# Query product from the transposed raw input and scaled afterwards, with the fourth layernorm's sums on ScalarE

## The reference, cut to what matters

```python
x = x + xattn(layernorm(x), ctx, ctx)      # q, k, v: relu(a @ W + b); relu(q k^T) / sqrt(512) + mask; relu(. @ v)
x = x + ffn(layernorm(x))                  # rows and weight quantised in blocks of 32 to a 6-bit float grid
x = x + mix(layernorm(x), ctx)             # x @ W1^T + mean part + b
x = x + experts(layernorm(x))              # 16 experts, each on the 128 tokens that its gate likes best
```

## Time and profile before

| | us |
|---|---|
| three runs | 745.37, 745.30, 744.03; median 745.3 |
| span of the profiled execution | 743.2 |
| PE busy | 716.2 (96%) |
| PEld busy | 624.9 (84%) |
| DVE busy | 521.6 (70%) |
| POOL busy | 420.4 (57%) |
| ACT busy | 401.9 (54%) |

### The profile page before, as it was taken

The page is one execution under the profiler, slowest core; times in us unless marked ns, Lnnn a source line. Parts: engine busy times, 40 slices in busy tenths (PEclk is TensorE's granted clock), DMA queues, the critical chain, the costliest instruction groups (busy, mean ns, idle before and its releaser), DMA issues.

```text
span 743.2 us, 12766 instructions
## 1 busy us (share of the span) xinstructions
PE 716.2 (96%) x4513; PEld 624.9 (84%) x4513; DVE 521.6 (70%) x978; ACT 401.9 (54%) x680; POOL 420.4 (57%) x621
## 2 busy tenths in 40 slices
...
GB/s 317 256 30 15 43 86 62 88 86 58 88 79 82 71 58 108 52 60 44 49 45 264 322 396 279 149 391 186 222 370 185 185 330 293 289 266 167 142 86 58
DMA packets 61671, 118.04 MB, mean 159 GB/s; under 512 B 6056, under 2 KB 7464, under 8 KB 61608
## 3 DMA queue, kind: packets, MB, share of 16 engines
...
...
## 4 chain that ended last, share of the span: by engine, by line
PE 84%; issue 6%; DMA 4%; DVE 3%; ACT 2%; POOL 1%; POOLq 0%; SPq 0%; DVEq 0%; ACTq 0%
PE bank L354 39%; PE banks L354 9%; PE bank L361 6%; PE bank L994 6%; PE banks L861 4%; PE banks L867 4%; DMA out<-y,ids 3%; PE banks L871 2%; PE banks L994 2%; PE banks L872 2%; PE banks L1423 1%; PE banks L1028 1%; PE bank L1318 1%; PE bank L1041 1%; DMA out<-x 1%
## 5 line engine op out<-in xcount | busy, mean ns | idle before, releaser
L2844 POOL DMA_INDIRECT out<-y,ids x24 | 46.1, 1922 | 157.4 <-DVE y L2555 155.5
L1973 DVE TENSOR_TENSOR w_l<-w_raw,w_h 128x2048 fp32r<-128x2048 f32 x35 | 80.1, 2291 | 63.2 <-ACT w_h L1496 49.4
L1961 DVE BATCH_NORM_STATS2 bn<-x 128x6 f32<-128x512 f32 x113 | 77.7, 688 | 8.2 <-DMA x<-x 5.4
L1496 ACT ACTIVATE w_h<-w_raw 128x2048 fp32r<-128x2048 f32 x36 | 68.5, 1918 | 7.2 <-DMA w_raw<-w 7.2
L1892 ACT ACTIVATE h<-bank,b 128x512 f32<-128x512 f32 x48 | 33.0, 688 | 62.5 <-PE bank L354 57.8
L1973 DVE TENSOR_TENSOR hT_l<-h,hT_h 128x512 fp32r<-128x512 f32 x48 | 33.0, 689 | 39.8 <-ACT hT_h L1898 37.7
L354 PE MATMUL bank<-tokT_h,w_h 128*128 128x256 f32 x188 | 55.1, 293 | 0.0
L2607 POOL TENSOR_SCALAR rstd<-mean_var 128x1 f32<-128x1 f32 x108 | 25.7, 238 | 50.9 <-DVE mean_var L1966 42.6
L354 PE MATMUL bank<-tokT_h,w_l 128*128 128x256 f32 x188 | 53.2, 283 | 0.0
L354 PE MATMUL bank<-tokT_l,w_h 128*128 128x256 f32 x188 | 53.2, 283 | 0.0
L354 PE MATMUL bank<-wf_h,xdT_h 128*128 128x512 f32 x128 | 52.6, 411 | 0.0
...
## 6 DMA issues: line engine op xcount, KB each, us to landing
...
x<-x SPq DMA_DIRECT2D x32, 256.0 KB, 2.7
out<-x SPq DMA_DIRECT2D x32, 256.0 KB, 2.0
xn<-xn SPq DMA_DIRECT2D x32, 256.0 KB
mask<-mask_t SPq DMA_DIRECT2D x8, 256.0 KB, 3.4
...
```

What stands on the lines that cost most here:

```text
L1496: act.activation(dst, src, ACT.Copy).then_inc(sem, 1)
L1961: dve.bn_stats(bn6[which][:, j % 2, :], src[:, :]).then_inc(sem_bn[which], 1)
L1973: dve.tensor_tensor(dst, src, hi_part, ALU.subtract).then_inc(sem, 1)
L2844: pool.indirect_dma_start(out=out_rows, out_offset=bass.IndirectOffsetOnAxis(ap=ids[:, r:r + 1], axis=0), in_=y[e % 2][b][:, :], in_offset ...
```

## The change

It uses that layernorm is a shift and a scale of each token. If the mean over its input features is taken out of each column of the query weight, the product of the raw `x` with it is the product of `x - mean` with the weight, and each token's 1/sqrt(var + eps) can be multiplied in afterwards.

- The host hands in `x` also transposed (`x_t`). SP loads it by groups (1 MB, 8 times) into the bytes of the low half of `xT1`. `xt_hi` (ACT, two instructions of 128x1024 per group, turns k % 4 = 0 and 1) makes the high part. The low part is made of three pieces of 128x512 on POOL (turns k % 4 = 0, 1, 2, behind `q_lo`) and one on DVE (k % 4 = 2); for groups 0 and 1 it is one instruction of 128x2048 on DVE. `t1`, `norm1`, `hi1`, `lo1` and six warm-up matmuls are gone.
- Four fp32 matmuls at the start give the weight's means, two DVE instructions subtract them.
- `rstd1` is made for four tiles at once (POOL, turns k % 4 = 1), written to DRAM and loaded back as a row on all partitions (`rb`). For group 0 this goes through PE and ACT.
- `scaled` (DVE, new, one per chunk) multiplies the product's bank by `rb` into `q32`; `q_relu` then works on `q32` in SBUF, high part first, then `q32` in place.
- `SUMMED` covers tiles 0 to 29: 22 tiles' sums move from DVE to ACT.
- In the loop, ACT's `hi2(k)` now stands ahead of `q_relu`, and POOL's `rstd4(k - 3)` behind `xd(k)` and `x1b(k)`, no longer ahead of them.
- At the start the DMAs, and the lists of steps on ACT, DVE and POOL, have another order (`wsum` is now ahead of the fourth `q_relu`).

The diff, cut to its core (from top to bottom: rules for all engines, SP, PE, ACT, DVE, POOL):

```diff
-    SUMMED = range(N - 10, N - 2)
+    SUMMED = range(0, N - 2)
...
+    def halves_of_group(k):
+        g, half = (k + 8) // GRP, k % GRP
+        return (g, half) if 2 <= g < G and half < 2 else None
+    def pool_piece(k):
+        g, c = (k + 8) // GRP, k % GRP
+        return (g, c) if 2 <= g < G and c < 3 else None
...
+        def load_xt(g):
+            if g >= 2:
+                sp.wait_ge(sm.p_q, GRP * (g - 1))
+            sp.dma_start(xt_raw[g % 2][:, :, :], chunked(io.x_t)[:, :, g * GT:(g + 1) * GT])\
+                .then_inc(sem_xt[g % 2], 16)
+        def store_r1(g):
+            sp.wait_ge(sm.g_r1, g + 1)
+            sp.dma_start(io.r1[g * GT:(g + 1) * GT].rearrange("(t p) -> p t", p=P), r1[:, g % 3, :],
+                         allow_slow_non_contiguous=True).then_inc(sm.r1_out, 16)
+        def load_rb(g):
+            sp.wait_ge(sm.r1_out, 16 * g)
+            sp.wait_ge(sm.d_z, GRP * g)
+            sp.dma_start(rb[:, :], rows_on_all(io.r1[g * GT:(g + 1) * GT], GT)).then_inc(sm.rb_in, 16)
...
-        def t1(j):
-            pe.wait_ge(sm.a_xn1, j + 1)
...
-            four_transposes(pe, bank1(j), xn1).then_inc(sm.p_t1, 1)
...
             if n == 0:
                 pe.wait_ge(sm.a_set, A["wq1"])
                 pe.wait_ge(sm.d_set, V["wq1"])
-            pe.wait_ge(sm.d_lo1, GRP * (g + 1))
+            pe.wait_ge(sm.d_xtl, g + 1)
+            if g >= 2:
+                pe.wait_ge(sm.g_xtl, 3 * (g - 1))
             if n >= 2:
-                pe.wait_ge(sm.a_q, n - 1)
+                pe.wait_ge(sm.d_z, n - 1)
             if n == 5:
...
+        def query_weight_means():
+            for d in range(C):
+                if d % 2 == 0:
+                    pe.wait_ge(sm.c_wq0 if d == 0 else sm.c_wq1, 16)
+                if d == 0:
+                    pe.wait_ge(sm.g_set, GS["mean"])
+                last = pe.matmul(ps_tb[:, :], mean_w[:, :], stage[0][:, d, :], start=(d == 0), stop=(d == C - 1))
+            last.then_inc(sm.p_set, 1)
+        def first_rows():
+            pe.wait_ge(sm.c_ident, 16)
+            pe.wait_ge(sm.g_r1, 1)
+            for t in range(GRP):
+                last = pe.transpose(ps_ta[:, t * P:(t + 1) * P], r1[:, 0, t:t + 1].to_broadcast([P, P]), ident[:, :])
+            last.then_inc(sm.p_set, 1)
...
-        t1(0)
-        warm_up(3)
...
+        query_weight_means()
...
+        first_rows()
...
-            if valid(k + 9):
-                t1(k + 9)
...
-        def norm1(j):
-            act.wait_ge(sm.p_t1, j)
-            norm(0, j, x_in[j % XR], xn1, sm.a_xn1, sm.g_r1)
...
-        def hi1(j):
...
-            hi(sm.a_hi1, xT1[j // GRP % 2][0][:, :, cols(j)], in4(bank1(j)))
+        def xt_hi(g, half):
+            act.wait_ge(sem_xt[g % 2], 16 * (g // 2 + 1))
+            part = slice(2 * half, 2 * half + 2)
+            hi(sm.a_xth, xT1[g % 2][0][:, part, :], xt_raw[g % 2][:, part, :])
...
         def q_relu(g, c, n):
...
-            act.wait_ge(sm.p_q, n + 1)
-            if n >= 2:
-                act.wait_ge(sm.g_qlo, n - 1)
-            act.activation(q32[n % 2][:, :], ps_q[n % 2][:, :], ACT.Relu, bias=bq[:, c:c + 1])
+            act.wait_ge(sm.d_z, n + 1)
             act.wait_ge(sm.p_s, g)
-            act.activation(q_h[:, c, :], ps_q[n % 2][:, :], ACT.Relu, bias=bq[:, c:c + 1]).then_inc(sm.a_q, 1)
+            act.activation(q_h[:, c, :], q32[n % 2][:, :], ACT.Relu, bias=bq[:, c:c + 1])
+            act.activation(q32[n % 2][:, :], q32[n % 2][:, :], ACT.Relu, bias=bq[:, c:c + 1]).then_inc(sm.a_q, 1)
...
         setup("k2")
         setup("k3")
+        setup("rb0")
         q_relu(*q_of(0))
-        hi1(4)
-        norm1(5)
+        xt_hi(1, 0)
         q_relu(*q_of(1))
-        hi1(5)
-        norm1(6)
+        xt_hi(1, 1)
         q_relu(*q_of(2))
-        hi1(6)
-        norm1(7)
+        setup("wsum")
         q_relu(*q_of(3))
-        hi1(7)
-        setup("wsum")
...
-            j = k + 9
-            if valid(j) and k >= 1:
-                hi1(j)
+            if halves_of_group(k) is not None:
+                xt_hi(*halves_of_group(k))
             if valid(k - 3) and not drain(k):
                 norm4(k - 3)
             g = scores_of(k)
             if g is not None and not scores_first(k):
                 s_relu(g)
-            if q_units(k):
-                q_relu(*q_units(k)[0])
             j = k
             if valid(j):
                 act.wait_ge(sm.p_t2, j + 1)
                 act.wait_ge(sm.p_f, j)
                 hi(sm.a_hi2, xd_h[:, :, :], in4(ps_tb))
+            if q_units(k):
+                q_relu(*q_units(k)[0])
             if fourth_later(k - 4):
...
-        def lo1(j):
-            i = j // GRP % 2
-            dve.wait_ge(sm.a_hi1, j + 1)
-            lo(sm.d_lo1, xT1[i][1][:, :, cols(j)], in4(bank1(j)), xT1[i][0][:, :, cols(j)])
+        def xt_lo(g):
+            dve.wait_ge(sm.a_xth, 2 * g + 2)
+            part = slice(0, C) if g < 2 else slice(C - 1, C)
+            lo(sm.d_xtl, xT1[g % 2][1][:, part, :], xt_raw[g % 2][:, part, :], xT1[g % 2][0][:, part, :])
+        def scaled(g, c, n):
+            dve.wait_ge(sm.p_q, n + 1)
+            if g == 0:
+                dve.wait_ge(sm.a_set, A["rb0"])
+            else:
+                dve.wait_ge(sm.rb_in, 16 * g)
+            if n >= 2:
+                dve.wait_ge(sm.g_qlo, n - 1)
+            dve.tensor_tensor(q32[n % 2][:, :], ps_q[n % 2][:, :], rb[:, :], ALU.mult).then_inc(sm.d_z, 1)
         def s_mask(g):
...
+        setup("wq0")
+        setup("wq1")
+        xt_lo(0)
         stats1(0)
         stats1(1)
         stats1(2)
         stats1(3)
-        lo1(0)
-        lo1(1)
-        lo1(2)
-        lo1(3)
         setup("wgc")
-        setup("wq0")
-        setup("wq1")
         stats1(4)
+        scaled(*q_of(0))
         stats1(5)
         setup("wf scales")
+        scaled(*q_of(1))
         stats1(6)
         stats1(7)
-        lo1(4)
         setup("wf8_0")
+        scaled(*q_of(2))
         setup("wf8_1")
-        lo1(5)
+        setup("wf8_2")
+        scaled(*q_of(3))
+        setup("wf8_3")
+        xt_lo(1)
         stats1(8)
         stats1(9)
-        lo1(6)
-        setup("wf8_2")
-        setup("wf8_3")
-        lo1(7)
         setup("va0")
         setup("v0")
         s_mask(0)
...
-            j = k + 9
-            if valid(j) and k >= 3:
-                lo1(j)
...
                 stats1(j)
+            if q_units(k):
+                scaled(*q_units(k)[0])
+            if k % GRP == 2 and 2 <= (k + 6) // GRP < G:
+                xt_lo((k + 6) // GRP)
...
+        def rstd1(g):
+            r, m = r1[:, g % 3, :], mv[0][:, GRP * g % 12:GRP * g % 12 + GRP, 1]
+            pool.wait_ge(sm.d_st1, GRP * (g + 1))
+            if g >= 4:
+                pool.wait_ge(sm.r1_out, 16 * (g - 3))
+            then(pool.tensor_scalar(r, m, LN_EPS, None, ALU.add))
+            pool.tensor_tensor(r, r, eps_exp[:, :].to_broadcast([P, GRP]), ALU.pow).then_inc(sm.g_r1, 1)
+        def xt_lo(g, c):
+            pool.wait_ge(sm.a_xth, 2 * g + 1 + c // 2)
+            lo(sm.g_xtl, xT1[g % 2][1][:, c, :], xt_raw[g % 2][:, c, :], xT1[g % 2][0][:, c, :])
...
-            if valid(k - 3) and not drain(k):
-                rstd_of(3, k - 3, sm.d_st4, sm.g_r4)
...
+            if valid(k - 3) and not drain(k):
+                rstd_of(3, k - 3, sm.d_st4, sm.g_r4)
...
                 s_lo(g)
-            if valid(k + 10):
-                rstd1(k + 10)
             if k == 1:
                 q_lo(*q_of(4))
             if not drain(k):
                 for unit in q_units(k):
                     q_lo(*unit)
+            if valid(k + 10) and (k + 11) % GRP == 0:
+                rstd1((k + 10) // GRP)
+            if pool_piece(k) is not None:
+                xt_lo(*pool_piece(k))
```

154 lines of the change are left out of this document (64 added, 90 removed).

## The result

The changed kernel takes 814.63 us (median of 4 runs, 810.57 to 816.94), the kernel before 745.04 in the same sessions: a ratio of 1.093, 95% interval [1.0896, 1.0958]. It is slower, as forecast, but by 69.6 us instead of 29, outside the range of 754 to 791.

The account below looks back on a forecast made before the run. PE bound the kernel before; a closed POOL-ACT-POOL chain would bind the changed loop. Span 743.2 + 2.8 (start) + 27.25 (five groups) - 1.5 (end) = 771.8, with 2.1 to the median 774 us; range 754 to 791.

Parts of the forecast that it names:

- the three waits named: Loop, turns 4 to 24: PE waits for POOL's xd, POOL for ACT's q_relu before q_lo, ACT for POOL's rstd4 before norm4.
- A: Rival for the loop: the chain has slack and PE remains the bound; 737.5 us, or 739.6 as a median; chance 0.10.
- B: Rival for the loop: the chain holds only in part, a group takes 45.3 to 47, time 747 to 755 us; chance 0.08.
- The chain of a plain turn: Loop, xd to next xd through POOL, ACT, POOL: 3.72 + 2.67 + 5.55 = 11.95 us, where PE needs 10.1.
- `xs64` 168.62 to 168.99 = 0.37: POOL, last step of the plain turn's chain: xs64 counts 0.37 us up to the next xd.
- the power on 128x4: POOL's rstd1 in turns k % 4 = 1: power taken as 1.1 us, with 0.4 for the addition, turn 13.45.
- The score turn: Turn k % 4 = 3: s_relu, mask, high part, sums and scaled stand ahead of q_relu; 13.4 us in all.
- 50.75: Group of four turns, 2 x 11.95 + 13.45 + 13.4 us instead of 45.30: 5.45 more, five times.
- The start: Before turn 4: first scores 4.2 us later, turns 1 to 3 give back 1.4; +2.8 at turn 4, bounds 0 and 7.
- I take half, 1.1: Start, DVE: second chunk's scaled behind the ffn weight's reductions, 2.25 us each, costs nothing or one; half taken.
- The end: From turn 24: the orders change, the chain ends, and t2(24) comes sooner after xd(24); -1.5 us.
- C: Rival: row rb, through DRAM, arrives 3 us late for a group's first chunk in five groups; 789 us; chance 0.07.

Follow-up runs that it names:

- e2_rstd4_ahead: Changed kernel, but on POOL rstd4(k-3) stands ahead of xs64 and xd again, ACT's order left as changed: 775.62 us, ratio 1.042.
- e8_mix_first: Changed kernel, but on POOL mix_bias stands ahead of rstd2, so it does not run beside DVE's scale: 832.07 us, one run.
- e4_start: Changed kernel, start reordered: second group's xt_hi and wsum behind q_relu, second scaled ahead of weight reductions, later q_lo ahead of dequantisation: 811.61 us, 1.091.
- e9_srelu_first: Changed kernel, but in score turns ACT does s_relu ahead of norm4 and not behind it: 805.67 us, ratio 1.082.
- e12_settled: Changed kernel with rstd4 and s_relu earlier, low-part pieces on DVE, start reordered, xt_hi at turn's end, sums of tiles 17 to 21 on DVE: 765.82 us, 1.029.

## Why the prediction was right or wrong

- **The bound and the side: right.** PE is no longer full, each of the three waits named stands where it was put, and cutting the chain at either end gives back 33 to 39 us. A (PE stays the bound) falls with these two runs, B (the chain holds only in part) with the group of 55.9. By size the span came out 40.4 us longer than the 771.8 of the sum: 24.5 of it lie in turns 4 to 23 (+51.7, past the upper bound of +38.5), 10.2 before them and 5.9 in turns 24 to 26.
- **The chain of a plain turn: right up to `xs64`, then mis-sized.** In turn 10 it is 6.79 to `q_lo` against 6.39, and 5.10 from there to `xs64` against 5.18; the power on 128x4 takes 1.04 to 1.05 (1.1 taken). The step that failed is "`xs64` 168.62 to 168.99 = 0.37": in each of the twenty turns `xd` comes 1.33 to 1.34 behind `xs64`, because it waits for DVE. That is 0.96 a turn and 19 us in all, the largest part of the miss. Before, the three instructions of `rstd4` stood between `mix_bias` and `xs64` and covered DVE's steps; the forecast took `xd` to depend on POOL alone there. With `rstd4` back in its place (e2_rstd4_ahead) most of these waits are gone. In the three turns without scores DVE is late since its scale takes 1.16 to 1.21 beside `mix_bias`; e8_mix_first shows that it is this neighbour.
- **The score turn: mis-sized by 1.0 to 3.3.** Up to `q_lo` turn 11 takes 9.04, as the sum had it (its terms add up to 9.2, not to the 9.1 that it gives). Behind `q_lo` the sum has `rstd2`, `mix_bias` and `xs64` with no wait; `mix_bias` waits 1.33 and `xd` 1.06, both at the end of a row that was in no term: `s_lo`, PE's wait of 4.36 for it, its attention product at the lower clock. With `s_relu` ahead of `norm4` four of these turns get 1.2 to 2.7 shorter and one 1.6 longer. On average the turns k % 4 = 0, 1, 2 and 3 are 0.9, 0.7, 1.3 and 2.4 longer than the sum had them, together the 5.1 by which a group missed its 50.75.
- **The start: +13.0 for +2.8, past the bound of 7.** The first scores come 7.46 later, where the sum had 4.2. The step that failed is "I take half, 1.1": the second `scaled` stood behind all of the reductions (it starts at 29.65, and at 27.41 in e4_start, which takes it ahead of them), and two more things were in no term, the load of the second group ahead of the second `q_relu`, and the dequantisation ahead of `q_lo`, 4.12 instead of 2.05 beside DVE's low part. From the scores to `xd(0)` another 2.6 went, near 2.2 of it since the twelve score matmuls step at the lower clock. Turns 0 to 3 took 3.0 more, where 1.4 was to come back; of this, turns 2 and 3 lose 2.6 less with `s_relu` ahead of `norm4` (e9_srelu_first). How much each wait of the start costs is read from the traces only: e4_start gave back 2.6 up to `xd(4)`, and the 5.8 of e12_settled come with edits to the loop.
- **The end: +4.4 for -1.5.** "In turn 24 the orders change" was wrong by a turn: 24 still has the loop's order, and 3.1 of the loss is that turn's chain, gone in e2_rstd4_ahead (whose turn 26 is 0.8 longer in exchange). The other 1.3 is in turns 25 and 26, where `q_lo` waits 0.92 and 0.74 for `q_relu`, which it did not before; no run took that away.
- **C: a late load, but not this one.** PE and DVE do not wait for the row `rb` in the loop; it is a 1 MB load of `x_t` at the start that is late.
- **What stays open.** The best version is still 21 us above the kernel before: 7.2 up to `xd(4)`, 6.5 in turns 4 to 23 and 5.6 in turns 24 to 26. In its first four groups PE is busy for 43.35 to 43.79 us at a granted clock of 1.00, so the 43.5 that the forecast gave PE is about right, and the group takes 45.5 to 46.7 all the same. Whether another order could win this saving was not found.
